# Ranking edges before a scatter: column counts taken ahead of the loop, in blocks of four columns

## The reference

```python
s2 = concat([src, dst]); d2 = concat([dst, src]); ef2 = concat([ef, ef])
for l in range(3):
    e_in = concat([h_prev[s2], h_prev[d2], ef2], axis=-1)
    msg = leaky_relu(e_in @ We1[l]) @ We2[l]
    red = segment_sum(msg, d2, num_segments=N)
    out = leaky_relu(concat([h_prev, red], axis=-1) @ Wn1[l]) @ Wn2[l]
    h_prev = out + h_prev
return layernorm(x + out)
```

## Time and profile before

| | us |
|---|---|
| median of 3 runs | 4590.27 |
| lowest and highest | 4588.41, 4593.47 |
| the profiled execution's own time | 4586.27 |
| its span, first to last instruction | 4584.5 |
| TensorE busy in the span | 3068.3 (67%) |
| VectorE busy | 2731.9 (60%) |
| ScalarE busy | 2204.1 (48%) |
| GpSimd busy | 816.0 (18%) |

### The profile page before, as it was taken

The page is one execution under the profiler, slowest core; times in us unless marked ns, Lnnn a source line. Parts: engine busy times, 40 slices in busy tenths (PEclk is TensorE's granted clock), DMA queues, the critical chain, the costliest instruction groups (busy, mean ns, idle before and its releaser), DMA issues.

```text
span 4584.5 us, 96167 instructions
## 1 busy us (share of the span) xinstructions
PE 3068.3 (67%) x30529; PEld 2550.2 (56%) x30530; DVE 2731.9 (60%) x6352; ACT 2204.1 (48%) x4081; POOL 816.0 (18%) x826
## 2 busy tenths in 40 slices
PE   3343333343432458888888878989889788988886
PEld 3343232233322356666666657777777577777774
DVE  7332222233324249999999976666666566666665
ACT  0100000111000246666666667777777677777774
POOL 0555555545555300000000000000000000000000
PEclk6555555555555669999999989999999899999998
DMA  6110000000100455666666634444444244444443
GB/s 195 29 29 21 21 21 21 21 24 25 29 21 5 105 127 186 216 205 213 211 207 216 204 122 160 155 158 159 161 154 162 84 162 151 162 160 153 162 151 113
DMA packets 196298, 559.29 MB, mean 122 GB/s; under 512 B 35602, under 2 KB 73176, under 8 KB 194232
## 3 DMA queue, kind: packets, MB, share of 16 engines
q1 hardware_dynamic: 168728, 543.70, 35.6%
q0 software_dynamic: 27552, 15.37, 1.8%
HBM read 401.38 MB, written 157.72 MB: 122 GB/s over the span
## 4 chain that ended last, share of the span: by engine, by line
PE 45%; DVE 10%; issue 9%; DMA 2%; ACT 1%; POOL 0%; DVEq 0%; ACTq 0%; SPq 0%; POOLq 0%
PE gath L1213 15%; PE sums L1268 12%; PE sums L1213 8%; PE gath L1206 5%; DVE loop_buf L971 3%; DVE loop_buf L988 3%; DVE big L902 2%; PE sums L1206 2%; DMA recc<-records 2%; PE sums L1118 1%; DVE gsel L906 1%; PE sums L1276 0%; PE sums L1138 0%; PE sums L1277 0%; PE sums L1282 0%
## 5 line engine op out<-in xcount | busy, mean ns | idle before, releaser
L902 DVE SCALAR_TENSOR_TENSOR big<-big 128x768 f32<-128x768 f32 (+1 forms) x957 | 907.1, 948 | 671.9 <-ACT big L669 631.6
L1213 PE MATMUL gath<-t_hi,gsel 128*128 x3744 | 944.2, 278 | 0.0
L1213 PE MATMUL gath<-t_lo,gsel 128*128 x3744 | 943.5, 278 | 0.0
L1268 PE MATMUL sums<-loop_buf 128*128 128x128 f16 x11232 | 792.5, 221 | 203.3 <-issue 202.7
L573 POOL DMA_INDIRECT records<-rec,rowi x784 | 790.3, 1008 | 641.2 <-DVE rec L843 399.3
L971 DVE TENSOR_TENSOR loop_buf<-big,loop_buf 128x768 f16<-128x768 f32 x936 | 889.3, 950 | 0.0
L1268 PEld LDWEIGHTS sums<-loop_buf 128*128 128x128 f16 x11232 | 678.5, 99 | 312.5 <-issue 185.7
L673 ACT ACTIVATE loop_buf<-big 128x768 f16<-128x768 f32 x936 | 782.2, 836 | 2.6
L669 ACT ACTIVATE big<-gath 128x512 f32<-128x512 f32 x936 | 559.5, 598 | 354.5 <-PE gath L1213 354.5
L614 ACT ACTIVATE numb<-sums 26x700 f32<-26x700 f32 x28 | 38.8, 1387 | 1268.2 <-remote 913.3
L664 ACT ACTIVATE big<-sums 128x256 f32<-128x256 f32 x936 | 355.4, 380 | 420.6 <-PE sums L1213 419.6
(11 more groups left out here) (168 smaller groups left out, 2681.3 us busy)
## 6 DMA issues: line engine op xcount, KB each, us to landing
gsel<-gsel_d SPq DMA_DIRECT2D x208, 576.0 KB, 3.8
loop_buf<-ssel_d SPq DMA_DIRECT2D x208, 576.0 KB, 5.2
numb<-nums_d SPq DMA_DIRECT2D x106, 576.0 KB, 4.7
gsel_d<-gsel SPq DMA_DIRECT2D x104, 576.0 KB, 5.6
ssel_d<-loop_buf SPq DMA_DIRECT2D x104, 576.0 KB, 6.5
fchunk<-feat_d SPq DMA_DIRECT2D x313, 144.0 KB, 2.9
loop_buf<-rows_d SPq DMA_DIRECT2D x28, 896.0 KB, 4.2
records<-rec,rowi POOLq DMA_INDIRECT x784
```

The costliest lines, as they stand in the source:

```text
L902: return dve.scalar_tensor_tensor(m, m, SLOPE, m, ALU.mult, ALU.max)
L1213: return pe.matmul(uv, gsel[:, h, (2 * tc + s) * P:(2 * tc + s + 1) * P], at[n], start=False, stop=n == 3, skip_group_check=True)
L1268: last = pe.matmul(out_n, m[:, place, w0:w0 + D], ssel[:, ts, s, :], start=False, stop=False, skip_group_check=True)
```

## The change

The counts of all columns are made ahead of the loop. The one-hot matrices are made for four columns at a time: 4 x 32 wide for the larger block, 4 x 25 for the smaller. One product of them holds the counts of the four columns as its diagonal blocks of 32 x 25 (the rest isn't used); a second product of the same operands adds to the totals. ScalarE copies the diagonal blocks to `cols`, which holds the counts of all 28 groups. The 28 columns of a group are four runs of 7 columns, one for each set of 32 partitions, and each set keeps its own chain of bases (`CHAINS`); a constant matrix `below` starts a chain where the one before it ends. The ranks' order within a bucket changes with that, which the result doesn't depend on but for rounding.

In the loop, `chain_bases` on DVE, one group ahead, sums the 7 columns of the four chains, adds the carry, and makes oat by comparing a row of block numbers, broadcast by four DMAs into `hrow`, with the partition's number in its set. The base is split into two fp16 parts, base/128 rounded (ScalarE, `base_high`) and the rest (DVE). TensorE then has 7 products of 128 x 128 with 200 columns for a group; DVE picks from 1,400 columns and joins the two parts.

```diff
-            def count_group(it, h):
...
-            pe.wait_ge(rowsT_set, 1)
-            count_group(0, 0)
+            with pe.Fori(0, GTURNS) as it:
+                for h in range(2):
+                    pe.wait_ge(cols_set, it * 2 + h - 1 + COLS_AHEAD)
+                    pe.wait_ge(hist_hot_set, it * 2 + h + 1)
+                    pe.sem_inc(pe_go, 1)
+                    for q in range(RUN):
+                        pe.matmul(sums[:, 2 * h * BANK + q * P:2 * h * BANK + q * P + CHAINS * NB], hot_hi[:, h, q, :],
+                                  hot_lo[:, h, q, :], start=True, stop=True, skip_group_check=True)
+                        last = pe.matmul(gath[:, 0:CHAINS * NB], hot_hi[:, h, q, :], hot_lo[:, h, q, :], start=False,
+                                         stop=False, skip_group_check=True)
+                    last.then_inc(hist_done, 1)
...
             with pe.Fori(0, GTURNS) as it:
                 for h in range(2):
                     pe.wait_ge(base_set, it * 2 + h + 1)
-                    pe.wait_ge(oat_set, it * 2 + h + 1)
+                    pe.wait_ge(found_set, it * 2 + h + AHEAD)
                     pe.sem_inc(pe_go, 1)
-                    for j in range(GROUP):
-                        last = pe.matmul(sums[:, 2 * BANK + j * SLOT:2 * BANK + j * SLOT + NB], oat[:, j * P:(j + 1) * P],
-                                         base3[:, :, j], start=True, stop=True, skip_group_check=True)
+                    for q in range(RUN):
+                        last = pe.matmul(sums[:, q * 2 * P:q * 2 * P + 2 * CHAINS * NB], oat[:, h, q * P:(q + 1) * P],
+                                         bases[:, h, q, :, :, :].rearrange("p k r b -> p (k r b)"), start=True, stop=True,
+                                         skip_group_check=True)
                     last.then_inc(base_ps, 1)
-                    if h == 0:
-                        count_group(it, 1)
...
+            with act.Fori(0, GTURNS) as it:
+                for h in range(2):
+                    act.wait_ge(hist_done, it * 2 + h + 1 + HIST_AHEAD)
+                    for r in range(CHAINS):
+                        at = slice(r * HW, (r + 1) * HW)
+                        last = act.activation(
+                            cols[at, ds(it * 2 + h, 1), :, 1:RUN + 1].rearrange("p g b s -> p (g s) b"),
+                            sums[at, 2 * h * BANK:2 * h * BANK + RUN * P].rearrange("p (q e) -> p q e", e=P)
+                            [:, :, r * NB:(r + 1) * NB], ACT.Copy)
+                    last.then_inc(cols_set, 1)
...
+            def base_high(group, h):
+
+                act.wait_ge(sum_set, group + 1)
+                for r in range(CHAINS):
+                    at = slice(r * HW, (r + 1) * HW)
+                    last = act.activation(bases[at, h, :, 0, r, :], base3[at, :, 0:RUN].rearrange("p b s -> p s b"), ACT.Copy,
+                                          scale=1.0 / P)
+                last.then_inc(base_hi_set, 1)
...
-                    act.wait_ge(counts_ps, it * 2 + h + 1)
...
-                    act.activation(oat[:, 0:OAT_A * P], sums[0:HI, 4 * BANK:4 * BANK + OAT_A * P // 2].bitcast(F16), ACT.Copy)
...
+                    if h == 0:
+                        base_high(it * 2 + 1, 1)
...
+            dve.memset(cols[:, :, :, 0], 0.0).then_inc(zeroed, 1)
+            dve.memset(bases.rearrange("p h q k r b -> p (h q k r b)"), 0.0).then_inc(zeroed, 1)
+            dve.memset(chain, 1.0).then_inc(zeroed, 1)
...
+            def chain_bases(group, turn, h):
+
+                dve.tensor_tensor_scan(prefix, chain, cols[:, ds(group, 1), :, :].rearrange("p g b s -> p (g b s)"), 0.0,
+                                       ALU.mult, ALU.add).then_inc(prefix_set, 1)
+                dve.wait_ge(prefix_set, group + 1)
+                dve.wait_ge(carry_set, group + 1)
+                dve.tensor_tensor(base3, prefix.rearrange("p (b s) -> p b s", s=RUN + 1),
+                                  carry.unsqueeze(2).to_broadcast([P, NB, RUN + 1]), ALU.add).then_inc(sum_set, 1)
+                dve.wait_ge(hrow_in[h], turn * (16 * CHAINS) + 16 * CHAINS)
+                dve.tensor_scalar(oat[:, h, :], hrow[:, h, :], part[:, 1:2], None, ALU.is_equal).then_inc(hrow_free, 1)
+                hot_lo_of(ob[:, h, :, :], group)
+                dve.wait_ge(sum_set, group + 1)
+                dve.tensor_copy(carry, base3[:, :, RUN]).then_inc(carry_set, 1)
+                dve.wait_ge(base_hi_set, group + 1)
+                for r in range(CHAINS):
+                    at = slice(r * HW, (r + 1) * HW)
+                    last = dve.scalar_tensor_tensor(bases[at, h, :, 1, r, :], bases[at, h, :, 0, r, :], float(-P),
+                                                    base3[at, :, 0:RUN].rearrange("p b s -> p s b"), ALU.mult, ALU.add)
+                last.then_inc(base_set, 1)
...
-                    dve.tensor_tensor_scan(base, chain[:, :], counts, 0.0, ALU.mult, ALU.add).then_inc(base_set, 1)
...
                     if h == 0:
-                        hot_group(it, 1)
+                        chain_bases(it * 2 + 1, it, 1)
...
             with sp.Fori(0, GTURNS) as it:
                 for h in range(2):
+                    col = (it * 2 + h) * GROUP
+                    sp.wait_ge(hrow_free, it * 2 + h - 1 + KROW_AHEAD)
+                    sp.sem_inc(sp_go, 1)
+                    for r in range(CHAINS):
+                        sp.dma_start(hrow[r * HW:(r + 1) * HW, h, :],
+                                     rows_d[1:2, ds(col + r * RUN, RUN), :].rearrange("k j p -> k (j p)")
+                                     .to_broadcast([HW, RUN * P])).then_inc(hrow_in[h], 16)
                     sp.wait_ge(krow_free, it * 2 + h - 1 + KROW_AHEAD)
```

More of the change, by code:

```diff
@@ L56 @@
 GTURNS = COLS // (2 * GROUP)
-HCOLS = 2 * GROUP
-SLOT = 32
+CHAINS = 4
+RUN = GROUP // CHAINS
+GROUPS = COLS // GROUP
+HW = P // CHAINS
+assert HI <= HW and CHAINS * RUN == GROUP
 ROWS = 112
 ROW_PARTS = COLS // ROWS
-OAT_A = 24
 MAPW = -(-(TURNS * STEPS + LAG) // P)
@@ L182, in build @@
         gsel_words = gsel[:, :, :].rearrange("p h e -> p (h e)").bitcast(F32)
-        pre_words = numb[:, :, :].rearrange("p h e -> p (h e)").bitcast(F32)[0:HI, 2 * COLS:PART * 2 * P]
-        counts = pre_words[:, 0:NB * (GROUP + 1)]
-        counts3 = counts.rearrange("a (b s) -> a b s", s=GROUP + 1)
         f_words = fchunk[:, :, :].rearrange("p h e -> p (h e)").bitcast(F32)
-        picked = f_words[:, 0:GROUP * NB].rearrange("p (j b) -> p j b", b=NB)
+        rowsT = f_words[0:ROWS, 0:2 * ROW_PARTS * P // 2].bitcast(F16).rearrange("r (k e) -> r k e", k=2)
+        oat = f_words[:, 0:RUN * P].bitcast(F16).rearrange("p (h e) -> p h e", h=2)
+        small = numb[:, :, :].rearrange("p h e -> p (h e)").bitcast(F32)[:, 2 * COLS:PART * 2 * P]
+        LINE = NB * (RUN + 1)
+        chain, prefix, base = (small[:, k * LINE:(k + 1) * LINE] for k in range(3))
+        carry = small[:, 3 * LINE:3 * LINE + NB]
+        base3 = base.rearrange("p (b s) -> p b s", s=RUN + 1)
         key = gsel_words[:, 0:COLS]
@@ L204, in build @@
         zeros16 = zeros[:, :].bitcast(F16)[:, 0:BUCKETS]
-        ones = sb("ones", [HI, P], F32)
-        chain = sb("chain", [HI, NB * (GROUP + 1)], F32)
+        ones = sb("ones", [P, P], F32)
+        below = sb("below", [P, P], F32)
+        own = sb("own", [P, HI], F32)
+        totals = sb("totals", [P, NB], F32)
+        beg_ab = sb("beg_ab", [P, NB], F32)
         map_f = sb("map_f", [P, MAPQ + 1, 2], F32)
@@ L598, in _ @@
                 act.sem_inc(s, AHEAD)
+            act.sem_inc(cols_set, COLS_AHEAD)
+            act.wait_ge(rowsT_ps, 1)
+            for k in range(2):
+                last = act.activation(rowsT[:, k, :], bank(4 + k)[0:ROWS, 0:ROW_PARTS * P // 2].bitcast(F16), ACT.Copy)
+            last.then_inc(rowsT_set, 1)
+            with act.Fori(0, GTURNS) as it:
[8 more added lines that the diff above has]
+                    last.then_inc(cols_set, 1)
             for n in range(BANKS):
@@ L747, in _, with by_run, numbers, hot_lo_of @@
-            with dve.Fori(0, COLS // (2 * HCOLS)) as it:
+            def by_run(t, group, width):
+                return t[:, ds(group * GROUP, GROUP)].rearrange("p (r q) -> p q r", r=CHAINS).unsqueeze(3)\
+                    .to_broadcast([P, RUN, CHAINS, width])
+            def numbers(width):
+                return iota[:, 0:width].unsqueeze(1).unsqueeze(1).to_broadcast([P, RUN, CHAINS, width])
+            def hot_lo_of(out, group):
+                return dve.tensor_tensor(out.rearrange("p q (r b) -> p q r b", b=NB), by_run(lo_b, group, NB), numbers(NB),
+                                         ALU.is_equal)
@@ new lines, in _ @@
+            dve.memset(cols[:, :, :, 0], 0.0).then_inc(zeroed, 1)
+            dve.memset(bases.rearrange("p h q k r b -> p (h q k r b)"), 0.0).then_inc(zeroed, 1)
+            dve.memset(chain, 1.0).then_inc(zeroed, 1)
+            dve.wait_ge(zeroed, 3)
```

(9 more changed lines are left out.)

208 lines of the change are left out of this document (99 added, 109 removed).

## The result

| | before | after |
|---|---|---|
| runs beside each other: median (lowest to highest), us | 4591.49 (4588.41 to 4593.47), 4 runs | 4415.06 (4413.44 to 4419.76), 4 runs |
| profiled execution: time, span, us | see above | 4413.44, 4411.7 |
| first scatter starts, last one ends, us | 122.43, 1523.32 | 173.72, 1350.06 |
| scatters' busy time, idle time before them, us | 790.3, 641.2 | 773.0, 439.4 |

The ratio is 0.9618, with a 95% interval of 0.9601 to 0.9635: 176 us faster by the medians, where 304 were forecast; the median lies 0.06 us above the upper end of the range given (4,415). The scatters end 173.3 us earlier and the span is 172.8 shorter, so the whole gain lies ahead of the end of the scatters. That stretch is the difference of two larger terms: the loop of scatters shrank from 1,400.9 to 1,176.3 us, by 224.6, and it begins 51.3 us later.

A forecast was written before the change was run, and what follows sets the result against it. GpSimd's scatters were taken as the bound, once the stop was gone: start 120 + scatters 988 + interference 99 + map 6 + back edges 6 = 1,219 against 1,523.3, 304 us less, so 4,282; range 4,220 to 4,415.

The forecast's parts named there:

- the long stop: GpSimd's wait between turns of two groups in the scatter loop, 28.6 us, with TensorE's late products ahead; forecast gone.
- Held signals: Rival, 0.06: TensorE's signal comes only after the scatters stop, stopping GpSimd 13.1 us each group; time 4,632.
- no effect: Rival, 0.02: the 28 us stop has another cause, such as an engine's loop restart, and stays; time 4,586.
- Full block: Rival, 0.05: GpSimd stands still through all of DVE's two-input work, 11.1 us more per group; time 4,494.
- Sum 17.6 us, half of the 35.3 that the scatters of a group last: DVE's work per group in the new loop, put at half the time of GpSimd's scatters.
- slack of 17 us: DVE's spare time per group beside the scatters, taken to cover the row loads' waits at no cost.
- the 99 and 6 allowed for interference and the map: Scatter slowing by DVE, 28 x 3.55 = 99 us, and ten scatters slowed by the end map (L849), 6 us.
- the 6 for the back edges: The loop's 13 back edges, formerly hidden in the stop, at 0.5 us each: 6 us (0 to 22).
- in proportion to what is queued: If TensorE trickles this way, its 7 products per group need some 20 us, costed at nothing.
- four times L614's 1,387 x 175/700 = 0.35, are 1.4, less than DVE's 1.75, so hidden; at 0.55 each they would lead: ScalarE's four diagonal-block copies per group ahead of the loop: hidden; if leading, 12 us more.
- the first scatter came after 140 us: Sign of being wrong, at the start of the scatter loop; the forecast start was about 120 us (117 to 137).
- a start of 137 and interference of 199: Upper-bound terms: latest first scatter, and all DVE work but the pick stopping GpSimd in full; with others, 4,415.

The follow-up runs named there:

- a4: Changed kernel with L879 as three instructions per group over all 28 columns: 4352.24 us, 1.0231 of the kernel before, which took 4252.92 beside it.
- f1: b3 with L879 without its accumulator, 28 instructions writing products in place and one sum behind: 4333.06 us beside the kernel before at 4251.27 (1.0192).
- b3: Changed kernel with counts stored blocks innermost, so ScalarE copies runs of 25 and VectorE turns them round later: 4343.72 us, 0.9458 of the kernel before.
- e1: Changed kernel with seven more TensorE products per group that nobody reads: 4410.04 us (one run), beside the kernel before at 4587.69.

## Why the prediction was partly right

**Right: the removed work had made the long stop.** In a session of the first kind TensorE's 84 products a group did make the stop of 28.6 us, and with 7 it is gone. Held signals, the rival by which TensorE's signal would come late however few its products are, fell with that: VectorE's L884, which takes these products, waited 5.9 us in all 28 groups together, and by the profile not for TensorE. So did no effect. Full block asked for 11.1 us of standstill a group; all scatters together show 773.0 - 784 x 0.96 = 20 us of stretching. Its mechanism is real all the same, as a4 and f1 show: it was L879's accumulator reads that kept it away, which the prediction did not see.

**Wrong by 77 us: VectorE's share of the loop.** The step that failed is "Sum 17.6 us, half of the 35.3 that the scatters of a group last", with the slack of 17 us that was built on it. The size was near what the work needs: 18.6 us, from 638.27 to 656.84, for the group that runs freely behind the stop above. But in the first kind of session the engine does not get its instructions at that rate beside scatters. The forecast loop was 1,219 - 120 = 1,099; measured were 1,176.3. The stops brought 158 us that the forecast did not have (439.4 of idle time, less 36.1 ahead of the first scatter, less 245.5 of pauses). Against that stretching and longer pauses came to 20 + 10 = 30 instead of the 99 and 6 allowed for interference and the map, and the 6 for the back edges were not needed: 158 - 75 - 6 = 77. I had read the trickle as TensorE's, "in proportion to what is queued", and did not ask what would happen to the next engine once its work had to run beside all scatters, not only beside those of every second group. The profile of before has no row that answers this: VectorE's L813 did not trickle there, but in the ninth turn it ran only 4 to 12 us after the scatters had resumed and in the stop, when TensorE was not held either.

**Wrong by 53.7 us: the start.** The step is "four times L614's 1,387 x 175/700 = 0.35, are 1.4, less than DVE's 1.75, so hidden; at 0.55 each they would lead". They took 0.94 and led, and the first scatter came after 140 us, one of the signs of being wrong that the prediction names. The step left out how the diff writes them: single 2-byte numbers, 16 bytes apart, which cost 5.4 ns each, where the same numbers in runs cost 1.8. That the 0.35 is near the 0.31 of the copy in runs is luck, as L614, which it was worked from, writes single numbers too, 4-byte ones 116 bytes apart, at 2.0 ns each. Whether the width or the distance makes the difference no run shows. (The first compare's 23.3 is short as well: 19.53, 1.2 and 3.4 make 24.1, and it began at 24.42.)

The two errors make 131 us, which is 1350.06 - 1219 = 131. That the time still came within 0.1 us of the upper bound is chance: the bound was made of a start of 137 and interference of 199, and holds no stop.

**Right only elsewhere.** Where nothing trickles, the forecast's loop is what the trace shows, GpSimd as the bound with 1,026.6 us. But there, by the estimate above and not by a trace, the kernel before comes near the same bound already, so the change has only some 37 us to win and loses 52 at the start. That the stops belonged to the session as much as to the kernel could not be read from one profile; the note that no row showed what makes TensorE trickle was the place to ask.

**What stays open.** That VectorE's number of instructions makes its stops is argued from the timeline; the runs that would have cut it (a4, f1) never met a session of the first kind, and b3, with one more a group, had shorter stops. e1 shows only that products of TensorE early after a restart change nothing. What differs between the sessions is not shown either. The missing landings point to the path on which events are recorded. The Trainium skill's NOTIFIC — the notification-queue block, section 7.1 (Overflow: three behaviours, one of which stalls the engine), says that the block's own pipeline holds its producers back rather than lose a record, and that stalls counted there would mean that the notification path had throttled an engine. By that, the landings beside the scatters could delay the engines' instructions, and a timing with records would be longer than one without; no run here shows that, since each was recorded, and it leaves open where the missing landings were lost.

## What to carry to other kernels

Price a small copy by how it writes, not only by its elements, and take the price from a copy with the same width and order: the same 175 numbers took 0.94 us scattered and 0.31 in runs, 112 times over. Where a trace shows "issue" waits that nothing explains, have the unchanged kernel run again in another session before building on them, and judge a change in both. And beside GpSimd's scatters, look whether VectorE's two-input instructions run without a break: here accumulator reads between them, or an instruction with one input, let the scatters pass.

## What the runs showed of the hardware that was not expected

- The same program on the same chip took 4,252 us in one session and 4,588 in another. For the changed kernel the traces show where: behind the last scatter both kinds need 3,062 to 3,066 us, and the loop of scatters takes 1,170 to 1,176 or 1,027.
- An unbroken row of two-input VectorE instructions (7.44 us) held one scatter for 4.95 us, in the next group for 6.00; with an accumulator read behind each instruction the scatters beside them take about 1.03.
- A compare of 128 x 3,584 with a 32-bit second input took 3.89 us, a multiply with a 16-bit one 2.02, both with 16-bit results.
